# One row of a 128-row gather moved from GpSimd to SyncE, in a one-core GNN layer

## Chip, core and metric

The kernel runs on one core of one Trainium2 chip. The metric is device time in microseconds (us), the median of several executions. The core has five engines that run their own instruction streams: TensorE (PE, with its weight loads shown as PEld), VectorE (DVE), ScalarE (ACT), GpSimd (POOL) and SyncE (SP). They wait for each other through semaphores. SP, ACT and POOL also start DMA transfers, which run on 16 DMA engines.

## What is computed

The layer has 100,000 nodes with 32 features (`x`) and 25,000 edges, each with a source node `src`, a target node `dst` (sorted), four numbers `edge_attr_4` and eight numbers `edge_attr_8`.

```python
h = jnp.maximum(_layernorm(x, axis=-1), 0.0)
# per edge: an MLP of edge_attr_8 gives four 8x8 weight blocks
e = jax.nn.silu(edge_radial @ W1 + b1); e = jax.nn.silu(e @ W2 + b2); tpw = e @ W3 + b3
# messages: products of h[src], edge_attr_4 and tpw, summed over 8
agg = jax.ops.segment_sum(messages, dst, num_segments=n_atoms) / np.sqrt(AVG_NEI)
# self part: h through Ws and Wv
x = x + (h_self + agg)
```

So there is a dense part over all nodes (norm, ReLU, a small matrix, add to `x`, store) and a sparse part over the edges: fetch `x[src]` for each edge, normalise it, build 32 numbers per edge, and add them to the rows `dst` of the output.

## The kernel before, in words

**Tiles of edges.** The edges are cut into 196 tiles, 128 edges on 128 partitions each; the last one has 40 (`T` = 195 whole tiles, `TAIL` = 40, L54 to L59). The fetched rows of `x` stand in SBUF in `xg`, 32 numbers per partition and tile.

**Node stage**, until about 158 us. SP loads chunks of 2,048 nodes (`load_x`, L219), PE, ACT and DVE work on them, ACT stores them. At the same time POOL gathers rows of `x` for the edges.

**Edge stage**, from then on. PE, ACT and DVE work in 49 batches of four tiles. A batch ends with DVE's `idx_i`, the row numbers (L973), and ACT's copy of the sums into one of four buffers `sums` (L464). POOL then scatters each of the batch's four tiles with an indirect DMA that adds into the output (`scatter`, L319 to L340).

**POOL's order** (L298 to L349) is written out by hand. It gathers tiles 0 to 156 one after the other (`GA` = 157, L316), waits for the dense stores, and then, for each batch q, gathers tile 157 + q while that is under `G1` and scatters batch q:

```python
for q in range(NQ):
    if GA + q < G1:
        gather(GA + q)
    scatter(q, q)
```

A batch's first scatter is tile 3 of it, then come tiles 2, 1 and 0. The first waits until tiles 3, 2 and 1 of the batch before have landed, the second until its tile 0 has. ACT may overwrite a `sums` buffer only when POOL has passed that second point of a batch (`landed`, L335).

**SP's rows.** The last eight tiles, 188 to 195 (`RT` = 8, `G1` = 188), are not gathered by POOL. SP fetches each of their rows, 936 in all, by a DMA of its own of 128 bytes (`gather_rows`, L275 to L287). It first loads the row numbers into `row_i`, one DMA per tile (L266 to L270), and reads 32 of them at a time into registers. During the node stage it fetches four rows after each chunk load from the 13th chunk on, 144 in all, and the other 792 behind the last load.

**Who waits for gathered rows.** The first 120 tiles (`GF` = 120) are used in groups of ten in the node stage. The later ones are used in groups of seven, `late_tiles(v)`: DVE waits for a group in `late_landed(v)` (L1020), just ahead of the sum over its rows (L840). For groups 0 to 9 that is in the third batch of pass v, batch 4v + 2; the last group, tiles 190 to 195, is waited for at batch 44.

Of the kernel before, what the change touches and what calls it, by code (L numbers as in the profile page):

```python
# [20 lines left out]
def gnn_layer(nc, x, src, dst, edge_sh, edge_radial, W1, b1, W2, b2, W3, b3, Ws, Wv, out):  # L21
    f32, bf16, i32 = mybir.dt.float32, mybir.dt.bfloat16, mybir.dt.int32
# [3 lines left out]
    ds = bass.ds  # L26

    P = 128
    N, D = x.shape
# [24 lines left out]
    T = E // P  # L54
    TAIL = E - T * P
# [8 lines left out]

    GT, GL, GA, RT = 10, 7, 157, 8
    G1 = T + 1 - RT
    EW = UT * NB
    GF = EARLY * GT  # L70
    LATE = NU // 2 - 1
    assert 0 <= GF + GL * LATE - (T + 1) <= 1
    DR = D + 1
# [6 lines left out]
    src_main = src[0:T * P].rearrange("(p t) -> p t", p=P)  # L80
# [3 lines left out]
    with ctx:  # L84
        def sb(name, shape, dt=f32):
            return ctx.enter_context(nc.sbuf_tensor(name, shape, dt))

        def sem(name):
            return ctx.enter_context(nc.semaphore(name))
# [33 lines left out]
        nstd = sb("nstd", [P, 2, R])  # L123
        nrstd = sb("nrstd", [P, 2, R])

        row_i = sb("row_i", [1, RT * P], i32)
        src_all = sb("src_all", [P, T + 1], i32)
        xg = sb("xg", [P, (T + 2) * D])
        gsum = sb("gsum", [P, GT])
# [68 lines left out]
        src_loaded, row_loaded = sem("src_loaded"), sem("row_loaded")  # L198
        gathered = [sem(f"gathered{i}") for i in range(EARLY)]
        gathered_late = [sem(f"gathered_late{i}") for i in range(LATE)]  # L200
        gathered_row = [sem(f"gathered_row{i}") for i in range(RT)]

        def rows(ap, c, base):

            _, p, r = CH[min(base, NCH - 1)]
            r0 = c * (P * R) if base < FULL else CH[base][0]
            return ap[ds(r0, p * r), :].rearrange("(p r) d -> p (r d)", p=p), p, r * D
# [3 lines left out]
        def late_tiles(j):  # L211
            return range(GF + j * GL, min(GF + (j + 1) * GL, T + 1))

# [3 lines left out]
        @block.sync  # L217
        def _(sp):
            def load_x(c, base):  # L219
                if base >= XS:  # L220

                    sp.wait_ge(s["o_done"], c - XS + 1)
                v, p, n = rows(x, c, base)
                sp.dma_start(xin[0:p, base % XS, 0:n], v).then_inc(x_loaded[base % XS], 16)

            sp.dma_start(src_all[:, 0:T], src_main).then_inc(src_loaded, 16)
            for c in range(2):
                load_x(c, c)
            sp.wait_ge(s["selfw_zero"], 1)
            sp.dma_start(wself32[0:MUL, 0:MUL], Ws).then_inc(s["selfw_loaded"], 16)  # L230
            for i in range(3):
                with nc.allow_non_contiguous_dma(reason="64 weights"):
                    sp.dma_start(wself32[MUL + i:D:3, MUL + i:D:3], Wv).then_inc(s["selfw_loaded"], 16)
            for c in range(2, 4):
                load_x(c, c)
            sp.wait_ge(s["selfw_scaled"], 1)
            for g in range(4):
                sp.dma_start(wself[g * D:(g + 1) * D, g * D:(g + 1) * D], wself32[:, :]).then_inc(s["selfw_placed"], 16)
            sp.wait_ge(s["zeroed"], 1)
            for k in range(4):  # L240

                sp.wait_ge(s["xT_ready"], k + 1)
                load_x(k + 4, k + 4)
                if k == 0:

                    for h in range(2):
                        sp.dma_start(b3f[:, h * NTP:(h + 1) * NTP], b3.rearrange("(a n) -> a n", a=1)).then_inc(s["w_loaded"], 16)
                        sp.dma_start(w3blk[h * HR:(h + 1) * HR, h * NTP:(h + 1) * NTP], W3).then_inc(s["w_loaded"], 16)
                if k == 1:
                    for h in range(2):  # L250
                        sp.dma_start(w2blk[h * HR:(h + 1) * HR, h * HR:(h + 1) * HR], W2).then_inc(s["w_loaded"], 16)
                        sp.dma_start(b1col[h * HR:(h + 1) * HR, :], b1.rearrange("(n a) -> n a", a=1)).then_inc(s["w_loaded"], 16)
                        sp.dma_start(b2col[h * HR:(h + 1) * HR, :], b2.rearrange("(n a) -> n a", a=1)).then_inc(s["w_loaded"], 16)
                if k == 2:
                    sp.dma_start(dst_i[:, 0:T], dst_main).then_inc(s["dst_loaded"], 16)
                    sp.dma_start(sh_all[:, 0:T * 4], sh_main).then_inc(s["sh_loaded"], 16)
                for t in (2 * k, 2 * k + 1):
                    sp.dma_start(w1big[t * NB:(t + 1) * NB, t // 2, (t % 2) * HR:(t % 2 + 1) * HR], W1)\
                      .then_inc(s["w_loaded"], 16)
            sp.dma_start(er_all[:, 0:T * NB], er_main).then_inc(s["er_loaded"], 16)  # L260
            sp.dma_start(er_all[0:TAIL, T * NB:(T + 1) * NB], edge_radial[T * P:E, :]).then_inc(s["er_loaded"], 16)
            sp.dma_start(sh_all[0:TAIL, T * 4:T * 4 + 4], edge_sh[T * P:E, :]).then_inc(s["sh_loaded"], 16)
            sp.wait_ge(s["dst_pad"], 1)
            sp.dma_start(dst_i[0:TAIL, T:T + 1], dst[T * P:E].rearrange("(n a) -> n a", a=1)).then_inc(s["dst_loaded"], 16)

            for t in range(G1, T + 1):  # L266
                n = P if t < T else TAIL
                rows_of = src_main[:, t:t + 1].rearrange("p a -> a p") if t < T else src_tail.rearrange("n a -> a n")
                with nc.allow_non_contiguous_dma(reason="128 row numbers"):
                    sp.dma_start(row_i[:, (t - G1) * P:(t - G1) * P + n], rows_of).then_inc(row_loaded, 16)  # L270
            sp.dma_start(out[N:N + BT * P, :].rearrange("(p r) d -> p (r d)", p=P), spare0[:, :]).then_inc(s["spare_stored"], 16)

            late_rows = iter([(t, p) for t in range(G1, T + 1) for p in range(P if t < T else TAIL)])
            nodes = []

            def gather_rows(count):

                for t, p in itertools.islice(late_rows, count):
                    if p % 32 == 0:
                        o = (t - G1) * P + p  # L280
                        w = min(32, (P if t < T else TAIL) - p)
                        _, numbers = nc.values_load_multi_w_load_instructions(
                            row_i[0:1, o:o + w], engines=[mybir.EngineType.SP], min_val=0, max_val=N - 1,
                            skip_runtime_bounds_check_because="src holds rows of x")
                        nodes[:] = numbers
                    sp.dma_start(xg[p:p + 1, t * D:(t + 1) * D], x[ds(nodes[p % 32], 1), :])\
                      .then_inc(gathered_row[t - G1], 16)  # L287

            for c in range(XS, NCH):
                load_x(c, c)  # L290
                if c == 12:
                    sp.wait_ge(row_loaded, 16 * RT)
                if 12 <= c < FULL:
                    gather_rows(4)
            gather_rows(P * RT)


        @block.gpsimd  # L298
        def _(pool):
# [10 lines left out]

            def gather(t):
                signal = gathered[t // GT] if t < GF else gathered_late[(t - GF) // GL]
                pool.indirect_dma_start(xg[:, t * D:(t + 1) * D], None, x,  # L313
                                        bass.IndirectOffsetOnAxis(ap=src_all[:, t:t + 1], axis=0)).then_inc(signal, 16)

            pool.wait_ge(src_loaded, 16)  # L316
            for t in range(GA):
                gather(t)
# [33 lines left out]
        def _(act):  # L352
# [192 lines left out]
            edge_pass(0, True, False, True)  # L545
            with act.Fori(1, LATE - 1) as v:
                edge_pass(v, False, False, True)
            edge_pass(LATE - 1, False, False, False)
            edge_pass(LATE, False, True, False)
            copy_sums(NQ - 2, NQ - 2)  # L550
# [188 lines left out]
        def _(dve):  # L739
# [280 lines left out]
            def late_landed(v):  # L1020
                tiles = late_tiles(v)
                dve.wait_ge(gathered_late[v], 16 * len([t for t in tiles if t < G1]))
                for t in tiles:
                    if t >= G1:
                        dve.wait_ge(gathered_row[t - G1], 16 * (P if t < T else TAIL))

            def edge_pass(v, first, last):
                n = EARLY + v
                t0 = GF + v * GL
                was, ww = ((EARLY - 1) * GT, GT) if first else (t0 - GL, GL)  # L1030
                for h in range(2):
# [8 lines left out]
                    for r in range(2):  # L1040
# [3 lines left out]
                        products(q, k, u)  # L1044
                        if h == 1 and r == 0 and v < LATE - 1:
                            late_landed(v)
# [74 lines left out]
```

## Time and profile before

| what | value |
|---|---|
| median of 3 runs | 618.04 us (617.47 to 618.76) |
| the profiled execution | 617.0 us |
| its span, first to last instruction | 615.0 us |
| busy: PE / DVE / ACT / POOL | 529.1 / 463.4 / 389.3 / 488.3 us |
| POOL's 196 scatters, 188 gathers | 305.7 us, 181.6 us busy |
| mean granted TensorE clock | 0.824 of full speed |

The span leaves out 2.0 us of the profiled execution's own time. A busy engine is not always the one that sets the end; the chain of waits tells which one does. DMA packets are counted per queue: q0 is the one that POOL's indirect DMAs use, q1 that of SP.

### The profile page before, as it was taken

The numbers are of one execution on the slowest core, as the hardware profiler recorded it, in microseconds if no ns is written. First come the engines' busy times: TensorE is split into PE (matmuls) and PEld (weight loads), VectorE is DVE, ScalarE is ACT, GpSimd is POOL, SyncE is SP. The second block draws the span as 40 slices with busy tenths as digits, with TensorE's granted clock in tenths as the row PEclk, the third lists the DMA queues.
The fourth block names the chain that finished last, engine by engine and source line by source line (L and its number), as shares of the span: only waits on it lengthen the run. The fifth ranks groups of instructions, "written<-read, shape, count | busy, mean of one in ns | idle before, by whom it ended". The sixth has DMA issues, their size and how long they took to land.

```text
span 615.0 us, 12788 instructions
## 1 busy us (share of the span) xinstructions
PE 529.1 (86%) x2843; PEld 394.7 (64%) x2867; DVE 463.4 (75%) x1125; ACT 389.3 (63%) x1103; POOL 488.3 (79%) x393
## 2 busy tenths in 40 slices
PE   6979999999799999888897998889899999987700
PEld 4768888888556666656664766566565666654600
DVE  4678889898489997777787777768877788857700
ACT  3426565656477977767596757757785778776400
POOL 6777777777777888888888888888888787888787
PEclk9959999999697887777888777778877778787755
DMA  4756667664200122222222222222222222222222
GB/s 129 193 184 185 203 195 203 207 204 141 82 14 15 12 11 12 11 10 10 12 11 11 11 10 13 9 11 10 12 10 11 11 8 10 10 10 9 10 9 9
DMA packets 53524, 34.36 MB, mean 56 GB/s; under 512 B 37062, under 2 KB 40920, under 8 KB 53464
## 3 DMA queue, kind: packets, MB, share of 16 engines
q0 software_dynamic: 34240, 6.32, 18.0%
q1 hardware_dynamic: 12054, 14.60, 8.2%
q10 hardware_dynamic: 7170, 12.81, 5.7%
q8 instruction: 18, 0.29, 0.2%
q14 instruction: 42, 0.34, 0.2%
HBM read 17.59 MB, written 16.08 MB: 55 GB/s over the span
## 4 chain that ended last, share of the span: by engine, by line
POOL 64%; issue 21%; DMA 14%; POOLq 0%
POOL out_dram L325 38%; POOL xg L313 25%; DMA out_dram<-sums,idx_i 14%; DMA src_all<-in_src_dram 0%; POOLq L335 0%; POOLq L341 0%; POOLq L342 0%; POOLq L331 0%
## 5 line engine op out<-in xcount | busy, mean ns | idle before, releaser
L325 POOL DMA_INDIRECT out_dram<-sums,idx_i x196 | 305.7, 1560 | 65.6 <-issue 54.4
L313 POOL DMA_INDIRECT xg<-in_x_dram,src_all x188 | 181.6, 966 | 58.4 <-issue 57.0
L645 PE MATMUL ps<-w3blk,x 128*128 128x512 f32 x196 | 142.5, 819 | 1.6 <-issue 0.4
L692 PE MATMUL ps<-msg,eq 128*128 128x32 f32 (+1 forms) x980 | 124.7, 287 | 1.8 <-DVE msg L1014 1.8
L692 PEld LDWEIGHTS ps<-msg,eq 128*128 128x128 f32 x980 | 124.4, 207 | 2.1 <-DVE msg L1014 2.0
L994 DVE TENSOR_REDUCE red<-prod 128x128 f32<-128x1024 f32 x49 | 97.8, 1996 | 0.1
L476 ACT ACTIVATE dsq<-ps,dcol 128x512 f32<-128x512 f32 x196 | 87.1, 537 | 0.2 <-PE ps L657 0.2
L464 ACT ACTIVATE sums<-ps 128x132 f32<-128x132 f32 x49 | 13.7, 279 | 111.6 <-POOLq L335 87.7
L645 PEld LDWEIGHTS ps<-w3blk,x 128*128 128x128 f32 x196 | 46.9, 253 | 44.4 <-issue 40.8
L498 ACT ACTIVATE eq<-dsq,onecol 128x384 f32<-128x384 f32 x147 | 73.4, 519 | 0.0
L657 PEld LDWEIGHTS ps<-ident,dcol 128*128 128x128 f32 x196 | 25.4, 151 | 59.1 <-issue 57.0
L596 PEld LDWEIGHTS ps<-ones_g,sqT 128*128 128x128 f32 x392 | 52.5, 202 | 12.8 <-issue 11.7
L602 PE MATMUL ps<-wself,rT 128*128 128x128 f32 x392 | 58.7, 295 | 0.0
L949 DVE SCALAR_TENSOR_TENSOR first<-sums,rank_max,dmt_all 128x4 f32<-128x4 f32 x49 | 10.8, 221 | 62.4 <-ACT sums L464 62.3
L376 ACT ACTIVATE sqT<-ps 128x512 f32<-128x512 f32 (+2 forms) x50 | 29.3, 585 | 44.4 <-PE ps L587 44.1
L981 DVE TENSOR_TENSOR prod<-ps,coef 128x768 f32<-128x768 f32 x49 | 46.8, 954 | 11.7 <-PE ps L646 9.3
L657 PE MATMUL ps<-ident,dcol 128*128 128x128 f32 x196 | 32.4, 292 | 26.1 <-ACT dsq L476 26.1
L985 DVE TENSOR_TENSOR prod<-ps,coef 128x256 f32<-128x256 f32 x147 | 52.8, 415 | 0.0
L1001 DVE TENSOR_REDUCE msg<-prod 128x32 f32<-128x512 f32 x49 | 52.5, 1072 | 0.0
L602 PEld LDWEIGHTS ps<-wself,rT 128*128 128x128 f32 x392 | 50.2, 200 | 0.1
L596 PE MATMUL ps<-ones_g,sqT 128*128 128x4 f32 x392 | 49.5, 249 | 0.4 <-DMA wself<-wself 0.4
L626 PE MATMUL ps<-erT,w1big 64*128 64x128 f32 x196 | 43.8, 389 | 3.7 <-ACT erT L404 3.1
(106 smaller groups left out, 803.9 us busy)
## 6 DMA issues: line engine op xcount, KB each, us to landing
xg<-in_x_dram SPq DMA_DIRECT2D x936, 0.1 KB
xin<-in_x_dram SPq DMA_DIRECT2D x48, 256.0 KB, 3.0
out_dram<-oc ACTq DMA_DIRECT2D x48, 256.0 KB, 2.3
out_dram<-sums,idx_i POOLq DMA_INDIRECT x196, 3.0
xg<-in_x_dram,src_all POOLq DMA_INDIRECT x188, 2.4
er_all<-in_edge_attr_dram SPq DMA_DIRECT2D x1, 780.0 KB
sh_all<-in_edge_attr_dram SPq DMA_DIRECT2D x1, 390.0 KB
xin<-in_x_dram SPq DMA_DIRECT2D x1, 192.0 KB, 3.1
```

What stands on the lines that cost most here:

```text
L313: pool.indirect_dma_start(xg[:, t * D:(t + 1) * D], None, x, bass.IndirectOffsetOnAxis(ap=src_all[:, t:t + 1], axis=0)).then_inc(signal, 16)
L325: pool.indirect_dma_start(out, bass.IndirectOffsetOnAxis(ap=idx_i[:, k % NS, a:a + 1], axis=0), sums[:, k % NS, a * DR:a * DR + D], None, ...
L476: m = act.activation(dsq[:, b * BW:b * BW + (BT - b) * P], psDT[:, b * P:BW], ACT.Square, bias=dcol[:, k % NS, b:b + 1], scale=-1.0)
L498: m = act.activation(e[:, o], dsq[:, o], ACT.Relu, bias=onecol[:, :], scale=-4.0, accum_out=lcnt[:, k % NS, b:b + 1])
L596: m = pe.matmul(psV[base % 2][0:p, 4 * g:4 * g + 4], sqT[:, base % 2, g * P:g * P + p], ones_g[:, :], start=True, stop=True)
L602: m = pe.matmul(psY[base % 2][0:p, g * P:(g + 1) * P], rT[:, base % 2, g * P:g * P + p], wself[:, :], start=True, stop=True)
L645: pe.matmul(o, x2[:, k // 2 % 2, j * P:(j + 1) * P], w3blk[:, :], start=True, stop=False)
L657: m = pe.transpose(psDT[:, b * P:(b + 1) * P], dcol[:, k % NS, b:b + 1].to_broadcast([P, P]), ident[:, :])
L692: m = pe.matmul(psSUM[:, a * DR:a * DR + n], eq[:, k % 2, o:o + P], msg[:, k % 2, b, 0:n], start=(b == a), stop=(b == a - 1 and (a < BT - ...
L985: m = dve.tensor_tensor(prod[:, :, 192 + 64 * i:256 + 64 * i].rearrange("p t (g w) -> p t g w", w=MUL), w[:, :, 192:256].rearrange("p t (g ...
L994: dve.tensor_reduce(red[:, :, :, :], prod[:, :, 128:384].rearrange("p t (g u w) -> p t g w u", u=MUL, w=MUL), X, ALU.add).then_inc(s["red_ ...
L1001: dve.tensor_reduce(msg[:, k % 2, :, 0:MUL], prod[:, :, 0:128].rearrange("p t (u w) -> p t w u", w=MUL), X, ALU.add)
```

## The change

Tiles 0 to 119 are gathered as before. From tile 120 on (the 121st), POOL's gather covers 127 partitions instead of 128. The 128th row of each of these tiles is fetched by SP, as a single-row DMA. SP's share of whole tiles shrinks from eight to seven (tiles 189 to 195), so POOL gathers tile 188 too: 189 gathers instead of 188, of which 69 have 127 rows. The 69 row numbers come with one more load into `row_i`; one load of 128 row numbers falls away. SP fetches the 69 single rows ahead of its whole tiles. SP has 877 rows in all. DVE has one more wait in `late_landed`.

```diff
-    GT, GL, GA, RT = 10, 7, 157, 8
+    GT, GL, GA, RT = 10, 7, 157, 7
     G1 = T + 1 - RT
     EW = UT * NB
     GF = EARLY * GT
+    ONES = G1 - GF
...
-        row_i = sb("row_i", [1, RT * P], i32)
+        row_i = sb("row_i", [1, RT * P + ONES], i32)
...
+        gathered_one = [sem(f"gathered_one{i}") for i in range(LATE)]
...
+            sp.dma_start(row_i[:, RT * P:RT * P + ONES], src_main[P - 1:P, GF:G1]).then_inc(row_loaded, 16)
+
+            ones = [(t, P - 1, RT * P, t - GF, ONES) for t in range(GF, G1)]
+            rows_of_tiles = [(t, p, (t - G1) * P, p, P if t < T else TAIL)
+                             for t in range(G1, T + 1) for p in range(P if t < T else TAIL)]
+            late_rows = iter(ones + rows_of_tiles)
...
-                for t, p in itertools.islice(late_rows, count):
-                    if p % 32 == 0:
+                for t, p, o, i, n in itertools.islice(late_rows, count):
+                    if i % 32 == 0:
...
-                    sp.dma_start(xg[p:p + 1, t * D:(t + 1) * D], x[ds(nodes[p % 32], 1), :])\
-                      .then_inc(gathered_row[t - G1], 16)
+                    sp.dma_start(xg[p:p + 1, t * D:(t + 1) * D], x[ds(nodes[i % 32], 1), :])\
+                      .then_inc(gathered_row[t - G1] if t >= G1 else gathered_one[(t - GF) // GL], 16)
...
-                    sp.wait_ge(row_loaded, 16 * RT)
+                    sp.wait_ge(row_loaded, 16 * (RT + 1))
...
-            gather_rows(P * RT)
+            gather_rows(ONES + P * RT)
...
-                pool.indirect_dma_start(xg[:, t * D:(t + 1) * D], None, x,
-                                        bass.IndirectOffsetOnAxis(ap=src_all[:, t:t + 1], axis=0)).then_inc(signal, 16)
+                n = P if t < GF else P - 1
+                pool.indirect_dma_start(xg[0:n, t * D:(t + 1) * D], None, x,
+                                        bass.IndirectOffsetOnAxis(ap=src_all[0:n, t:t + 1], axis=0)).then_inc(signal, 16)
...
                 dve.wait_ge(gathered_late[v], 16 * len([t for t in tiles if t < G1]))
+                dve.wait_ge(gathered_one[v], 16 * len([t for t in tiles if t < G1]))
```

## Rows read from the trace of the kernel before

**Rows 1.** The page: the span's chain that ended last, shares by engine.

```profile
POOL 64%; issue 21%; DMA 14%; POOLq 0%
```

**Rows 2.** Timeline of POOL: start us, length us, what [idle before <-releaser]. Early gathers.

```profile
194.71 0.95 POOL L313 DMA_INDIRECT xg<-in_x_dram,src_all  x1 [0.30 <-issue]
195.97 0.95 POOL L313 DMA_INDIRECT xg<-in_x_dram,src_all  x1 [0.30 <-issue]
...
202.28 1.63 POOL L325 DMA_INDIRECT out_dram<-sums,idx_i  x1 [0.30 <-issue]
```

**Rows 3.** Timeline of POOL: one batch, from its gather to the next scatter.

```profile
218.59 1.02 POOL L313 DMA_INDIRECT xg<-in_x_dram,src_all  x1 [0.30 <-issue]
219.91 1.57 POOL L325 DMA_INDIRECT out_dram<-sums,idx_i  x1 [0.30 <-DMA out_dram<-sums,idx_i]
221.79 1.56 POOL L325 DMA_INDIRECT out_dram<-sums,idx_i  x1 [0.30 <-issue]
223.66 1.56 POOL L325 DMA_INDIRECT out_dram<-sums,idx_i  x1 [0.30 <-issue]
...
227.37 1.02 POOL L313 DMA_INDIRECT xg<-in_x_dram,src_all  x1 [0.30 <-issue]
```

**Rows 4.** Timeline of POOL: the first batch without a gather, and the last scatter.

```profile
471.45 1.55 POOL L325 DMA_INDIRECT out_dram<-sums,idx_i  x1 [0.30 <-issue]
473.31 1.55 POOL L325 DMA_INDIRECT out_dram<-sums,idx_i  x1 [0.30 <-issue]
475.70 1.55 POOL L325 DMA_INDIRECT out_dram<-sums,idx_i  x1 [0.84 <-issue]
...
611.52 1.55 POOL L325 DMA_INDIRECT out_dram<-sums,idx_i  x1 [0.30 <-issue]
```

**Rows 5.** Waits between 210 and 470 us: who for whom, total us, times, longest.

```profile
ACT sums L464 <- POOLq L335: 70.9, 29, 3.6
```

**Rows 6.** The page: DMA queue of POOL's indirect DMAs: packets, MB, share of 16 engines.

```profile
q0 software_dynamic: 34240, 6.32, 18.0%
```

**Rows 7.** Timeline of POOL: its smallest instruction, a fill of one column.

```profile
0.26 0.10 POOL L1109 MEMSET const-float32-0.0<- 128x1 f32 x1 [0.26 <-issue]
```

**Rows 8.** Timeline of DVE: the row numbers of batches 0, 1 and 2.

```profile
185.83 0.16 DVE L973 TENSOR_TENSOR idx_i<-idx_f,trash 128x4 int32<-128x4 f32 x1
...
197.20 0.15 DVE L973 TENSOR_TENSOR idx_i<-idx_f,trash 128x4 int32<-128x4 f32 x1
...
204.64 0.16 DVE L973 TENSOR_TENSOR idx_i<-idx_f,trash 128x4 int32<-128x4 f32 x1
```

**Rows 9.** Stretches: window, us, busy PE, PEld, DVE, ACT, POOL, granted clock, DMA share, GB/s.

```profile
175.00:180.00 5.00, 4.64 (x23) 2.62 (x21) 4.93 (x8) 3.72 (x9) 3.78 (x5) 1.00 0.08 13
...
210.00:470.00 260.00, 238.39 (x1120) 167.03 (x1133) 205.62 (x508) 188.69 (x560) 214.86 (x149) 0.80 0.23 11
```

**Rows 10.** Gathers and their readers: what touches xg (duration min/median/max ns, first and last start), and landing.

```profile
L313 POOL DMA_INDIRECT xg<-in_x_dram,src_all x188: 947/952/1189, 3.1 to 464.5; - x188
L840 DVE TENSOR_REDUCE gsum<-xg x12: 374/377/428, 157.2 to 537.9; 128x7 f32<-128x224 f32 x11, 128x10 f32<-128x320 f32 x1
...
DMA to landing us min/median/max: 2.2/2.4/3.3
```

**Rows 11.** Timeline of DVE: row sums of group 0 and of group 9.

```profile
187.78 0.37 DVE L840 TENSOR_REDUCE gsum<-xg 128x7 f32<-128x224 f32 x1
...
490.49 0.38 DVE L840 TENSOR_REDUCE gsum<-xg 128x7 f32<-128x224 f32 x1
```

**Rows 12.** Timeline of SP's queue: number loads, the 18th four rows, the last 792.

```profile
23.16 6.31 SPq L270 DMA_DIRECT2D row_i<-in_src_dram  x8
...
88.85 1.46 SPq L286 DMA_DIRECT2D xg<-in_x_dram  x4
...
141.92 382.85 SPq L286 DMA_DIRECT2D xg<-in_x_dram  x792
```

More of the change, by code:

```diff
@@ L271, in _ @@
             sp.dma_start(out[N:N + BT * P, :].rearrange("(p r) d -> p (r d)", p=P), spare0[:, :]).then_inc(s["spare_stored"], 16)
-            late_rows = iter([(t, p) for t in range(G1, T + 1) for p in range(P if t < T else TAIL)])
+            sp.dma_start(row_i[:, RT * P:RT * P + ONES], src_main[P - 1:P, GF:G1]).then_inc(row_loaded, 16)
[3 more added lines that the diff above has]
+            late_rows = iter(ones + rows_of_tiles)
             nodes = []
             def gather_rows(count):
-                for t, p in itertools.islice(late_rows, count):
-                    if p % 32 == 0:
-                        o = (t - G1) * P + p
-                        w = min(32, (P if t < T else TAIL) - p)
+                for t, p, o, i, n in itertools.islice(late_rows, count):
+                    if i % 32 == 0:
+                        w = min(32, n - i)
                         _, numbers = nc.values_load_multi_w_load_instructions(
-                            row_i[0:1, o:o + w], engines=[mybir.EngineType.SP], min_val=0, max_val=N - 1,
+                            row_i[0:1, o + i:o + i + w], engines=[mybir.EngineType.SP], min_val=0, max_val=N - 1,
                             skip_runtime_bounds_check_because="src holds rows of x")
                         nodes[:] = numbers
-                    sp.dma_start(xg[p:p + 1, t * D:(t + 1) * D], x[ds(nodes[p % 32], 1), :])\
-                      .then_inc(gathered_row[t - G1], 16)
+                    sp.dma_start(xg[p:p + 1, t * D:(t + 1) * D], x[ds(nodes[i % 32], 1), :])\
+                      .then_inc(gathered_row[t - G1] if t >= G1 else gathered_one[(t - GF) // GL], 16)
             for c in range(XS, NCH):
```

## The prediction

> **What bounds the kernel now.** I read the chain of waits first. It runs through POOL nearly from end to end: 64% are POOL's own instructions and 21% the gaps between them, and the DMA part of 14% is the landing of scatters, which mostly runs beside POOL's next instructions [rows 1]. PE is busier in sum (529.1 us against 488.3), but sums don't tell which engine ends last, so I looked at POOL's timeline. In the first 200 us it is one gather after the other, 0.95 us each and 0.30 us to the next, so one gather every 1.26 us [rows 2]. Then a batch is one gather and four scatters, 1.32 us and 4 x 1.87 us, together 8.78 us from gather to gather, again with no more than the 0.30 us between instructions [rows 3]. There are 31 such batches, then 18 without a gather, until the last scatter starts at 611.52 [rows 4]. The other engines run ahead and are held back by POOL: between 210 and 470 us ACT waits 29 times, 70.9 us in all, until POOL frees a buffer [rows 5], some 2.4 us a batch. So a microsecond taken from POOL's sequence should be a microsecond of the kernel, as long as that reserve lasts, and one added costs one.
>
> **The change, part by part.**
>
> *The tile that POOL takes over (188).* It is gathered ahead of batch 31. At today's price that is 1.32 us [rows 3]. Batch 31 now idles 0.84 us ahead of its second scatter, 0.54 us more than the usual 0.30 [rows 4]: it waits for the scatter started at 471.45 to land. A gather in between covers that. Net +0.8 us.
>
> *The 69 gathers of 127 rows.* They are tiles 120 to 188: 37 in the early sequence and 32 ahead of batches 0 to 31. No row shows a gather of 127 rows. If the price goes by rows, each saves 1/128 of 0.95 us, 0.007 us, 0.5 us in all. What may change more is how the transfer is split. The queue has 34,240 packets [rows 6]; 188 gathers of 32 packets and 196 scatters of 144 make exactly that number. So I read a gather as 16 packets with 8 rows each and 16 small ones that signal the end, one of each per DMA engine, and a scatter as 128 row packets and 16 signals. 128 rows divide into 16 equal shares; 127 is a prime, so a program that wants equal shares must put all rows on one DMA engine. POOL would then prepare one list, not sixteen.
>
> Bounds for a gather: it can't cost less than POOL's smallest instruction, 0.10 us [rows 7], a saving of 0.85 us; above, I take the scatter, 1.56 us for the same 128 rows handled as separate packets [rows 3], 0.61 us more than a gather. Between these ends I choose an estimate. The scatter's 0.61 us over 128 rows is 4.8 ns per row for handling a row on its own. If the basic work on a row is about as much, 128 rows take 0.61 us of the gather; 0.10 us is the floor of any instruction; 0.24 us of the 0.95 are left for setting up 16 lists, 15 ns each. One list instead of 16 then saves 15/16 of 0.24 us, and with the row about **0.23 us a gather**. 69 x 0.23 = 15.9 us.
>
> The trace's packet count can't tell what 127 rows do. [...]
>
> *Landing of a gather on one DMA engine.* Between 175 and 180 us only gathers and single rows move: a DMA share of 0.08 of 16 engines, 6.4 engine-us for four gathers, at most 1.6 each [rows 9]. All on one engine, that adds 1.6 us to a landing of 2.4 [rows 10]. Group 9, the one with the tightest distance, is summed by DVE at 490.5 us [rows 11], and its last POOL gather would start at 473 us at today's pace: nobody waits. If instead the rows went as single packets like the scatter's: 0.23 x 16 x 260 us over 29.6 batches is 32 engine-us a batch [rows 9], some 8 for each scatter of 144 packets, 0.056 us a packet, so 7.1 us on one engine. A scatter behind it on that engine would land late. The scatter that must have landed by the next batch's first one starts 5.1 us after the gather, the next batch's first scatter 10.1 us after it; the rows would be through by some 8 us. Cost nothing; if a row took over 0.07 us, POOL would wait.
>
> *SP.* One number load more and one less, 0.79 us each [rows 12], in a stretch where SP waits for DVE anyway. 69 rows come first and fit in the 144 that SP fetches during the node stage (the 18 groups of four that they take are through at 90.3 us [rows 12]); their first reader, the sum of group 0, runs at 187.8 us [rows 11]. In all SP has 877 rows, not 936. 733 are left at 141.9 us, at 382.85/792 = 0.483 us each: SP ends at 496 us, not 525 [rows 12]. The last group is summed at 537.9 us [rows 10], some 15 us earlier after the change: 27 us of reserve, against 13 us before. Cost nothing.
>
> *DVE's added wait.* Eleven waits on semaphores that were raised long before; what stands behind them on DVE is a row sum of 0.38 us [rows 10]. Under 0.1 us each, and DVE is not the bound.
>
> *Does POOL find its work?* The early savings bring it to its first scatter 38 x 0.23 = 8.7 us earlier, 193.5 instead of 202.28 [rows 2]; the row numbers of batch 0 are there at 186.0 [rows 8]. Batch 1's scatters then begin at 202.1 (numbers at 197.4), batch 2's at 210.6 (204.8). Batches of 8.55 us leave ACT 2.2 us of its 2.4 us wait. Up to 0.3 us a gather nothing is lost here. At 0.5 us POOL would reach its first scatter at 183.3 and wait 2.7 us for batch 0 and 3.2 us for batch 1.
>
> *Sum:* +0.8 - 15.9 = -15.1 us. 617.0 - 15.1 = 601.9 us for the profiled execution; the median stands 1.0 us above that one, so **603 us**.
>
> **Rivals.**
>
> (a) *The price goes by rows.* For it: nothing in the trace shows a set-up per DMA engine. Then the added tile and 69 x 0.007 us nearly cancel: +0.3 us, 618.3. Chance 0.15.
>
> (b) *127 rows take a slower path on POOL, and the kernel is slower.* 128 rows over 16 engines may be the case for which POOL's program works on 16 lists at once; 127 rows on one list, or in unequal shares, would be handled row by row. For it: the scatter, which costs 0.61 us more for the same rows, so a slower path exists. Against: what is slow there may be the adding. Place: each of the 69 gathers, 37 of them before the first scatter. Price up to 69 x 0.61 = 42 us: 617.0 + 0.8 + 42.1 = 659.9, with the 1.0 us **661 us**. It decides from 0.03 us a gather on, where 69 x 0.03 and the 0.8 make 2.9 us. Chance 0.25, with anything between 620 and 661 us or beyond.
>
> (c) *The gathers get much cheaper and the gain stops at the other engines.* With 0.5 us a gather: +0.8 - 34.5 + 5.9 = -27.8 us, 590 us, the rest lost in the two waits for row numbers. Against more: PE is busy 92% of the 260 us at a clock of 0.80 [rows 9]. Chance 0.1.
>
> **How the numbers follow.** The forecast has 0.5, rival (c) 0.1, (a) 0.15 and (b) 0.25. A change under 0.2%, 1.2 us, can't be told from none here. Of (a) some lands on either side: faster 0.60, same 0.13, slower 0.27. The range must leave out no more than 0.2: it takes in (c) at 590 with a little below, 587, the forecast and (a), and the beginning of (b), up to 0.1 us a gather dearer, 618 + 0.8 + 6.9 = 626. What is left out is most of (b).
>
> **What would show it.** In the profile after: POOL's 69 gathers of tiles 120 on at about 0.72 us early and 0.79 later, the 120 others at 0.95. Queue q0 with fewer packets for them. Batch to batch 8.55 us, first scatter near 193.5 us, SP's last row near 496 us, no wait of DVE ahead of the sums of `xg`. If those gathers show 0.95 us, (a) holds; over that, (b); if POOL idles ahead of batches 0 and 1 for `idx_i`, (c). The forecast is wrong in another way if the gathers are cheaper and the batches still take 8.8 us, with POOL waiting for landings.

## The result and the profile after

The kernel became slower, by 127.8 us: a median of 745.7 us (744.65 to 746.25, 4 runs) against 617.94 us. The ratio is 1.2058, with a 95% interval from 1.2039 to 1.2078. The forecast was 603 us, the range ended at 626 us, and the rival on the slow side was priced at up to 661 us.

The page of the kernel after: its span, the chain's shares, then POOL's two groups of instructions (busy us, mean ns, idle ahead of them). Lines of this kernel are shifted: the scatter is L333, the gather L321, and L343 is where POOL signals that a buffer is free.

```profile
span 743.5 us, 12621 instructions
POOL 68%; issue 27%; DMA 4%; POOLq 0%
L333 POOL DMA_INDIRECT out_dram<-sums,idx_i x196 | 306.6, 1564 | 66.4 <-issue 61.7
L321 POOL DMA_INDIRECT xg<-in_x_dram,src_all x189 | 291.9, 1545 | 74.9 <-issue 73.0
```

The chain still runs through POOL, as it did before [rows 1]. The scatters cost nearly what they did (305.7 us before), but the gathers went from 181.6 to 291.9 us busy. POOL's timeline shows where. First the last 128-row gather and the first two with 127 rows (tiles 120 and 121), then the seventh of these and the eighth (tiles 126 and 127), then the first scatter:

```profile
153.08 0.95 POOL L321 DMA_INDIRECT xg<-in_x_dram,src_all  x1 [0.30 <-issue]
154.34 2.56 POOL L321 DMA_INDIRECT xg<-in_x_dram,src_all  x1 [0.30 <-issue]
157.20 2.55 POOL L321 DMA_INDIRECT xg<-in_x_dram,src_all  x1 [0.30 <-issue]
...
171.68 2.54 POOL L321 DMA_INDIRECT xg<-in_x_dram,src_all  x1 [0.31 <-issue]
177.84 2.55 POOL L321 DMA_INDIRECT xg<-in_x_dram,src_all  x1 [3.62 <-issue]
...
279.01 1.65 POOL L333 DMA_INDIRECT out_dram<-sums,idx_i  x1 [0.30 <-issue]
```

A gather of 127 rows takes 2.54 us, one of 128 rows 0.95 us. In the batches they take 2.59 and 1.02 us. Besides, POOL stands still for 3.6 us instead of 0.30 ahead of tile 127, and again ahead of 134, 141, 148 and 155. The first scatter starts at 279.01 us, not 202.28 [rows 2]. One batch, in the rows that answer to [rows 3]:

```profile
286.56 2.59 POOL L321 DMA_INDIRECT xg<-in_x_dram,src_all  x1 [0.30 <-issue]
289.47 1.59 POOL L333 DMA_INDIRECT out_dram<-sums,idx_i  x1 [0.32 <-issue]
...
296.96 2.59 POOL L321 DMA_INDIRECT xg<-in_x_dram,src_all  x1 [0.30 <-issue]
```

10.4 us from gather to gather instead of 8.78, and no stalls here.

So the 128.5 us by which the span grew are these. The 38 slow gathers ahead of the first scatter: 38 x 1.59 = 60.4. The 31 behind it: 31 x (2.59 - 1.02) = 48.7. Five stalls, 16.3 us together. Tile 188 at its old price, 1.3 us by a run below. That makes 126.7; 1.8 us are left over, about half of it in scatters that are a little longer (306.6 us in all, not 305.7) and the rest in small gaps.

What the other engines did meanwhile: the longest waits (who for whom, total us, times, longest), and the stretch from 210 to 260 us (busy us of PE, PEld, DVE, ACT, POOL, then clock, DMA share, GB/s).

```profile
ACT sums L472 <- POOLq L343: 219.4, 39, 67.9
DVE first L957 <- ACT sums L472: 188.4, 42, 66.1
```

```profile
210.00:260.00 50.00, 0.10 (x1) 0.00 (x0) 0.00 (x0) 0.00 (x0) 39.06 (x16) 0.53 0.38 8
```

ACT's wait for POOL in [rows 5] was 70.9 us; here ACT once waits 67.9 us in one piece. The three compute engines filled the four buffers and then did next to nothing for these 50 us, with POOL alone at work.

The queue q0, and SP's last fetches (start, length, count):

```profile
q0 software_dynamic: 37584, 6.85, 25.7%
```

```profile
141.34 379.54 SPq L293 DMA_DIRECT2D xg<-in_x_dram  x733
```

The packets tell how a gather is made. In the trace of the kernel before, q0's packets have three sizes: 3,008 of 1,024 bytes, which is 16 for each of 188 gathers, with 8 rows of 128 bytes in each; 25,088 of 128 bytes, 128 for each of 196 scatters; and 6,144 of 4 bytes, 16 for each of the 384 transfers. In 35 of the 37 gathers of tiles 120 to 156 a 4-byte one is the last packet ahead of the next gather, and the last of the 16 steps of the gather's semaphore stands 0.28 to 0.64 us behind the last 4-byte one (30 gathers, those with all 16 steps in the trace), so the 4-byte ones are read as signals.

In the kernel after, 120 gathers of 32 packets and 196 scatters of 144 leave 5,520 packets for the 69 gathers of 127 rows, 80 each. By their sizes these 80 are (bytes; the second column is how they are read):

```
3 x 4096, 1 x 3968   : 127 rows of 128 bytes, in packets of 32, 32, 32 and 31
45 x 128, 15 x 124   : 15 times 127 pieces of 4 bytes, in packets of 32, 32, 32 and 31
16 x 4               : the 16 signals
```

A sixteenth of the packets that are not signals, four of 64 here, is called a list, and a row or a 4-byte piece in it an entry. One list holds all rows: its four packets come one behind the other, and in none of the 69 gathers do two of them overlap by more than 7 ns, while of the 124-byte packets up to 15 are under way at once. The trace does not name the DMA engine of a packet, so the prediction's "one of each per DMA engine" and its one engine for 127 rows are shown only as far as these times go. The sizes of the others read as 15 lists filled up to the same length of 127 with pieces of 4 bytes. The profile shows packets and not the pieces in them, so the 4 bytes are inferred from the sizes. The bytes agree: q0 moved 0.53 MB more than in [rows 6], 7.7 KB for each of 69 gathers, and 15 x 127 x 4 bytes are 7.6 KB. Where a 128-row gather has 8 entries in each of 16 lists (1,024 bytes each), this one has, by this reading, 127 in each of 16.

### The profile page after: what moved, and what is told of

Read it like the earlier page. It is cut to its first block, busy times and chain, and to the rows that moved or that the text cites. A ratio compares the mean times of both kernels' runs of the same rounds, so it can differ in the third digit from the quotient of the medians.

```text
span 743.5 us, 12621 instructions
## 1 busy us (share of the span) xinstructions
PE 567.2 (76%) x2843; PEld 425.7 (57%) x2867; DVE 464.1 (62%) x1125; ACT 389.2 (52%) x1103; POOL 599.5 (81%) x394
## 4 chain that ended last, share of the span: by engine, by line
POOL 68%; issue 27%; DMA 4%; POOLq 0%
POOL out_dram L333 35%; POOL xg L321 33%; DMA out_dram<-sums,idx_i 4%; DMA src_all<-in_src_dram 0%; POOLq L343 0%; POOLq L349 0%; POOLq L339 0%; POOLq L350 0%
## 5 line engine op out<-in xcount | busy, mean ns | idle before, releaser
L333 POOL DMA_INDIRECT out_dram<-sums,idx_i x196 | 306.6, 1564 | 66.4 <-issue 61.7
L321 POOL DMA_INDIRECT xg<-in_x_dram,src_all x189 | 291.9, 1545 | 74.9 <-issue 73.0
L653 PE MATMUL ps<-w3blk,x 128*128 128x512 f32 x196 | 146.9, 842 | 2.1 <-issue 1.1
L700 PEld LDWEIGHTS ps<-msg,eq 128*128 128x128 f32 x980 | 145.6, 237 | 2.1 <-DVE msg L1022 1.8
L700 PE MATMUL ps<-msg,eq 128*128 128x32 f32 (+1 forms) x980 | 145.3, 312 | 1.6 <-DVE msg L1022 1.1
L665 PE MATMUL ps<-ident,dcol 128*128 128x128 f32 x196 | 35.2, 310 | 119.3 <-ACT dsq L484 119.3
L653 PEld LDWEIGHTS ps<-w3blk,x 128*128 128x128 f32 x196 | 48.9, 264 | 47.7 <-issue 44.1
L634 PE MATMUL ps<-erT,w1big 64*128 64x128 f32 x196 | 46.9, 411 | 3.4 <-ACT erT L412 3.1
```

The source lines that it names most:

```text
L321: pool.indirect_dma_start(xg[0:n, t * D:(t + 1) * D], None, x, bass.IndirectOffsetOnAxis(ap=src_all[0:n, t:t + 1], axis=0)).then_inc(signa ...
L333: pool.indirect_dma_start(out, bass.IndirectOffsetOnAxis(ap=idx_i[:, k % NS, a:a + 1], axis=0), sums[:, k % NS, a * DR:a * DR + D], None, ...
L653: pe.matmul(o, x2[:, k // 2 % 2, j * P:(j + 1) * P], w3blk[:, :], start=True, stop=False)
L665: m = pe.transpose(psDT[:, b * P:(b + 1) * P], dcol[:, k % NS, b:b + 1].to_broadcast([P, P]), ident[:, :])
L700: m = pe.matmul(psSUM[:, a * DR:a * DR + n], eq[:, k % 2, o:o + P], msg[:, k % 2, b, 0:n], start=(b == a), stop=(b == a - 1 and (a < BT - ...
```

## The experiments

All of them start from the kernel before. Those with fewer rows per gather leave SP's part as it was before (eight whole tiles, no single rows). The rows left out stay at zero in `xg`, so their share of the edges is computed from zeros. For that DVE clears these tiles at the start, and POOL waits for it once, at the latest ahead of the first of them. The diffs leave these lines out, and so they do added semaphores and DVE's waits for them.

**rt7_only: only the eighth tile moved.** `RT = 7`, all gathers with 128 rows.

```diff
-    GT, GL, GA, RT = 10, 7, 157, 8
+    GT, GL, GA, RT = 10, 7, 157, 7
```

> The kernel before with SP's whole tiles cut from eight to seven and nothing else: POOL gathers 189 tiles, all with 128 rows. Both theories: the added gather costs 1.32 us less the 0.54 us of idle time ahead of batch 31's second scatter that it covers, so +0.8 us, 618.7 us against 617.9. If it costs over 3 us, a part of the 128 us of the change is not in the 127-row gathers.

Measured: 619.1 us against 617.8, ratio 1.0025 (1.0010 to 1.0039), 1.3 us more. POOL's timeline where the added gather stands:

```profile
473.65 1.02 POOL L313 DMA_INDIRECT xg<-in_x_dram,src_all  x1 [0.30 <-issue]
474.97 1.57 POOL L325 DMA_INDIRECT out_dram<-sums,idx_i  x1 [0.30 <-DMA out_dram<-sums,idx_i]
476.85 1.56 POOL L325 DMA_INDIRECT out_dram<-sums,idx_i  x1 [0.30 <-issue]
```

The gather costs 1.32 us with its gap, and the 0.84 us ahead of the second scatter is gone, as said. The interval of the ratio is 0.6 to 2.4 us and takes in the expected 0.8, so whether the 0.54 us of covered idle time were won can't be told. Moving the tile is about 1% of the loss.

**no_single_rows: 127 rows without SP's part.**

```diff
+                n = P if t < GF else P - 1
...
-                pool.indirect_dma_start(xg[:, t * D:(t + 1) * D], None, x,
-                                        bass.IndirectOffsetOnAxis(ap=src_all[:, t:t + 1], axis=0)).then_inc(signal, 16)
+                pool.indirect_dma_start(xg[0:n, t * D:(t + 1) * D], None, x,
+                                        bass.IndirectOffsetOnAxis(ap=src_all[0:n, t:t + 1], axis=0)).then_inc(signal, 16)
```

> The kernel before with POOL's 68 gathers from tile 120 on cut to 127 rows; SP fetches eight whole tiles as before and no single rows, so the last row of those tiles is left at zero. Theory A (the change's loss is all in POOL's preparation of 127-row gathers): 2.54 and 2.59 us a gather instead of 0.95 and 1.02, five stalls of 3.3 us among the first 37, one such gather fewer than in the change: 745.7 - 2.9 + 0.5 = 743 us, within 2 us. Theory B (SP's single-row DMAs or their landings take part in it): under 738 us.

Measured: 741.35 us (739.75 to 744.97), ratio 1.2017 (1.1985 to 1.2050). The loss is there without a single-row DMA. This run has one slow gather fewer than the change, 2.9 us. Of the 4.35 us between the two medians some 1.5 us are then left for SP's 69 rows and all else, and runs that spread from 739.75 to 744.97 us don't tell that from nothing.

**row_counts: ten sizes in one trace.**

```diff
+    COUNTS = 4 * [112] + 4 * [120] + 4 * [126] + 4 * [125] + 4 * [124] + 4 * [96] + 4 * [64] + 3 * [127] + 3 * [122] + 3 * [32]
...
+                n = COUNTS[(t - GF) % len(COUNTS)] if t >= GF else P
```

> One trace with many sizes: from tile 120 on POOL gathers, in turn, 4 tiles each of 112, 120, 126, 125, 124, 96 and 64 rows, then 3 each of 127, 122 and 32; the rows above are left at zero. Theory A (the rows go in k equal lists, k the largest number up to 16 that divides them, and POOL pays 13.4 ns per entry of the longest list, from 2.54 - 0.95 us over 127 - 8 entries): 112 rows 0.94 us, 120 (15 lists of 8) 0.95, 126 (14 of 9) 0.97, 125 (5 of 25) 1.18, 124 (4 of 31) 1.26, 96 0.93, 64 0.90, 127 2.54, 122 (2 of 61) 1.66, 32 0.87 us. Theory B (any number that 16 does not divide takes a path that handles each row by itself): 120, 122, 124, 125, 126 and 127 all between 2.4 and 2.6 us, the others near 0.95. Stalls of 3.3 us: by A none, since the lists stay short.

POOL's timeline, one row for each size: 112, 120, 126, 125, 124, 96, 64, 127, 122 and 32 rows in this order.

```profile
156.66 0.92 POOL L317 DMA_INDIRECT xg<-in_x_dram,src_all  x1 [0.30 <-issue]
...
160.79 0.97 POOL L317 DMA_INDIRECT xg<-in_x_dram,src_all  x1 [0.30 <-issue]
...
165.90 0.99 POOL L317 DMA_INDIRECT xg<-in_x_dram,src_all  x1 [0.30 <-issue]
...
169.75 1.18 POOL L317 DMA_INDIRECT xg<-in_x_dram,src_all  x1 [0.30 <-issue]
...
177.30 1.27 POOL L317 DMA_INDIRECT xg<-in_x_dram,src_all  x1 [0.30 <-issue]
...
182.24 0.91 POOL L317 DMA_INDIRECT xg<-in_x_dram,src_all  x1 [0.30 <-issue]
...
189.55 0.91 POOL L317 DMA_INDIRECT xg<-in_x_dram,src_all  x1 [0.30 <-issue]
191.97 2.55 POOL L317 DMA_INDIRECT xg<-in_x_dram,src_all  x1 [0.30 <-issue]
...
200.52 1.66 POOL L317 DMA_INDIRECT xg<-in_x_dram,src_all  x1 [0.30 <-issue]
...
206.41 0.87 POOL L317 DMA_INDIRECT xg<-in_x_dram,src_all  x1 [0.30 <-issue]
```

The whole kernel took 632.5 us, measured once. Theory A gave 0.94, 0.95, 0.97, 1.18, 1.26, 0.93, 0.90, 2.54, 1.66 and 0.87 us. All ten rows shown are within 0.02 us; 128 and 127 rows had gone into the law, the other sizes had not. Of the 27 other gathers of these sizes ahead of the batches two stand out, at 1.36 us (120 rows) and 1.48 us (124 rows), and in the batches a gather costs some 0.05 us more, as it does at 128 rows. Theory B, a slow path for every number that 16 does not divide, needed 2.4 us or more at 120 and 126 rows, where 0.97 and 0.99 us were measured, and fell. The packet sizes in this trace agree with the number of lists. A list is one packet, at 122 rows two (packets x bytes for one gather, without the signals):

```
rows  with rows                 filler
128   16 x 1024 (8 rows)
120   15 x 1024 (8 rows)         1 x 32
126   14 x 1152 (9 rows)         2 x 36
125    5 x 3200 (25 rows)       11 x 100
124    4 x 3968 (31 rows)       12 x 124
122    2 x 4096, 2 x 3712 (61)  14 x 128, 14 x 116
```

A list of filler has in each case 4 bytes for every row in a list of rows. Gathers of 112, 96, 64 and 32 rows have 16 packets of 896, 768, 512 and 256 bytes. Of the packets with rows at most 5 were under way at once at 125 rows, 4 at 124 and 2 at 122.

**rows_122: a second price on the same line, in the whole kernel.** The edit of no_single_rows with `n = 122` from tile 120 on.

> POOL gathers 122 rows from tile 120 on (two lists of 61), the rows above left at zero, eight whole tiles on SP. If POOL pays per entry of the longest list, each of the 68 gathers costs 1.66 us, 0.71 us more than at 128 rows: 48 us, 617.8 + 48 = 666 us without stalls. If seven 127-row gathers stall because 7 x 128 entries fill something, gathers of 62 entries stall after each 14th, ahead of tiles 134 and 148, some 6 us: 672 us. If the stalls come with the change of the semaphore once gathers are slow: ahead of 127, 134, 141, 148 and 155, some 16 us: 682 us.

Measured: 666.9 us against 617.4, ratio 1.0802 (1.0767 to 1.0837): 49.5 us more, where 68 x 0.71 = 48 us were expected, and no stall where the other two readings put one. The 15th of these gathers, tile 134:

```profile
181.93 1.66 POOL L316 DMA_INDIRECT xg<-in_x_dram,src_all  x1 [0.30 <-issue]
```

122 rows cost 50 us and 127 rows cost 124. So the number of rows has little to do with it; the length of the lists has: 1.66 us a gather with 61 entries, 2.54 with 127.

**The stalls.** They are 16 us of the loss. The profile names nothing that releases POOL there (its word is `issue`). Five runs, all with 127 rows, changed where the slow gathers begin, or which semaphore they signal.

*start_at_123*: `n = P if t < GF + 3 else P - 1`.

> 127 rows only from tile 123 on, the last row of those tiles left at zero, eight whole tiles on SP. It tells apart what the stalls of 3.3 us after each seventh gather hang on. Theory A (the room of the descriptor lists: seven gathers fill it): the first stall stands ahead of tile 130, then 137, 144, 151. Theory B (the change of the semaphore, which comes with each group of seven tiles): ahead of tiles 127, 134, 141, 148, 155. Gathers 120 to 122 at 0.95 us. Time by A about 743 - 3 x 1.6 - one stall of 3.3 = 735 us.

Measured once: 733.5 us. No stall ahead of tile 127 and none ahead of 130; the first stands ahead of 134, behind eleven slow gathers, then every seven:

```profile
186.49 2.54 POOL L316 DMA_INDIRECT xg<-in_x_dram,src_all  x1 [0.31 <-issue]
193.18 2.54 POOL L316 DMA_INDIRECT xg<-in_x_dram,src_all  x1 [4.15 <-issue]
```

Neither theory was right as put.

*two_semaphores*: 127 rows from tile 120 on; the first three gathers of a group signal one semaphore, the other four another.

```diff
-                signal = gathered[t // GT] if t < GF else gathered_late[(t - GF) // GL]
+                signal = gathered[t // GT] if t < GF else (gathered_late if (t - GF) % GL < 3 else gathered_tail)[(t - GF) // GL]
```

> 127 rows from tile 120 on, last row left at zero, eight whole tiles on SP, and in each group of seven the first three gathers signal one semaphore and the other four another. If a change of the semaphore makes POOL stall: stalls ahead of tiles 123, 127, 130, 134 and so on, some ten of 3.3 us, 741 + 17 = 758 us. If it is a matter of how much has been put into the lists: stalls ahead of 127, 134, 141, 148, 155 as before, 741 us.

Measured once: 727.4 us, no stall at all, though the same entries went into the same lists. More changes of the semaphore made fewer stalls. Both expectations missed again. POOL's gathers of tiles 126 and 127:

```profile
175.05 2.55 POOL L317 DMA_INDIRECT xg<-in_x_dram,src_all  x1 [0.30 <-issue]
177.91 2.54 POOL L317 DMA_INDIRECT xg<-in_x_dram,src_all  x1 [0.30 <-issue]
```

*start_at_116*: `n = P if t < GF - 4 else P - 1`.

> 127 rows from tile 116 on, last row left at zero, eight whole tiles on SP, semaphores as they were (groups of ten below tile 120, of seven above). If the stalls count what has been put into the lists, the pattern of seven moves: with 11 gathers between tile 123 and the stall ahead of tile 134 in the run that started there, and 7 in the ones that started at 120, what counts is a running total over all gathers, and the stalls need not stand ahead of 127, 134, 141. If they hang on the groups: ahead of 120 or 127, then 134, 141, 148, 155. Four more slow gathers, 4 x 1.6 us: 741 + 6 = 747 us, one stall more or less 3.3 us.

Measured once: 747.1 us, as expected by the count of gathers. No stall ahead of 120, and none ahead of 123, the eighth slow gather; the first one stands ahead of 127, behind eleven slow gathers, then every seven:

```profile
183.91 2.55 POOL L316 DMA_INDIRECT xg<-in_x_dram,src_all  x1 [3.51 <-issue]
```

*cut_groups*: the groups are cut at 6, 5, 7, 6, 5.

> 127 rows from tile 120 on as in the run with two semaphores, but the groups of seven are cut at other places: 6 + 1, 5 + 2, 7 (uncut), 6 + 1, 5 + 2, later ones 4 + 3. So far a stall of 3.3 us stood behind each run of seven slow gathers on one semaphore (change, tiles 120 on) and behind none of 3 + 4. If it takes seven in a row on one semaphore: one stall only, behind the uncut group, ahead of tile 141, 727.4 + 3.3 = 731 us. If six are enough: also ahead of 126 and 147, 737 us; if five: four or five stalls, 741 us or more. If none stands anywhere, the link to the semaphores is wrong.

Measured once: 728.2 us. POOL's rows ahead of tile 127 (6 + 1), tile 141 (the uncut group) and tile 148 (6 + 1):

```profile
175.02 2.55 POOL L318 DMA_INDIRECT xg<-in_x_dram,src_all  x1 [0.95 <-issue]
...
218.04 2.54 POOL L318 DMA_INDIRECT xg<-in_x_dram,src_all  x1 [3.47 <-issue]
...
238.32 2.54 POOL L318 DMA_INDIRECT xg<-in_x_dram,src_all  x1 [0.66 <-issue]
```

The full stall, 3.47 us, stands behind the uncut group alone. Behind 6 + 1 there is a rest of it, 0.95 and 0.66 us, and behind 5 + 2 nothing, 0.30 us. The rest ends 6.34 us after the sixth gather started (168.68), which is about what the full stalls have after their seventh (171.68 to 177.84 is 6.16).

Landings show what ends these waits. In the kernel after, tile 126's gather started at 171.68 us and had landed 5.4 us later, at 177.10, and POOL went on at 177.84; behind its other four stalls POOL went on 0.60 us after the seventh gather's landing. In cut_groups it went on 0.71 us after the landing of the sixth gather (174.31) and not of the seventh (176.94, after POOL had gone on), which signals another semaphore. In all 22 waits of the kernel after, no_single_rows, start_at_123, start_at_116 and cut_groups, POOL went on 0.58 to 0.74 us after the last gather of the seven, or of the six, that signal one semaphore had landed. Where the run is shorter, it has landed before POOL gets there: in two_semaphores the third gather, tile 122, had landed at 166.29 us, and tile 127 started at 175.05 with the usual 0.30 us ahead of it.

A count fits all these places: seven gathers of 127 rows may stand in it and not eight; ahead of the eighth, the oldest run of gathers that signal one semaphore must have landed, and then leaves the count as a whole. That the count is one of room in the lists is the author's guess; no run shows it. In the batches, where no stall stands, scatters with other semaphores stand between the gathers, 10.4 us from one to the next. One run was made to test the count ahead of the fact.

*start_at_110*: `n = P if t < GF - 10 else P - 1`.

> 127 rows from tile 110 on, last row left at zero, eight whole tiles on SP; tiles 110 to 119 are one group of ten on one semaphore, then groups of seven. Two readings of the stalls. Room: the lists hold seven gathers of 127 rows (7 x 128 entries) and not eight, and POOL gets room back for whole runs of gathers that signal one semaphore, as far as they have landed; this fits all runs so far. Then seven gathers fill the lists in the middle of the group of ten: a stall ahead of tile 117, none ahead of 120 or 124, then ahead of 127, 134, 141, 148, 155; six stalls, and ten more slow gathers than from 120 on: 741.4 + 16 + 3 = 760 us. Bound: the stall belongs to the change of the semaphore: ahead of 120 and not ahead of 117, the others the same.

Measured once: 760.1 us. The rows around tiles 116 and 117, in the middle of the group of ten, and around 126 and 127:

```profile
158.73 2.54 POOL L316 DMA_INDIRECT xg<-in_x_dram,src_all  x1 [0.31 <-issue]
165.18 2.54 POOL L316 DMA_INDIRECT xg<-in_x_dram,src_all  x1 [3.91 <-issue]
...
191.50 2.54 POOL L316 DMA_INDIRECT xg<-in_x_dram,src_all  x1 [0.30 <-issue]
197.56 2.54 POOL L316 DMA_INDIRECT xg<-in_x_dram,src_all  x1 [3.52 <-issue]
```

The stall is where the count reaches eight, ahead of 117, with no change of the semaphore there, and none stands ahead of 120 or 124. The forecast of place and time held, and the six waits again end 0.60 to 0.74 us after the landing of the last gather before them. What POOL counts inside is not shown; the count is inferred from these places.

## Why the prediction was wrong

**What bounds the kernel: right, as far as it was put to the test.** POOL set the end before and after, and each microsecond added to its sequence was one of the kernel: 109 us of slower gathers and 16 us of stalls are 125 of the 128 us. Whether a microsecond taken away would have come out in full, no run shows.

**The tile that POOL takes over: right in place and gap.** +0.8 us was put down, 1.3 measured, with 0.8 inside the interval.

**The price of a 127-row gather: wrong, and this is the step that failed.** The prediction took the 0.95 us apart into 128 rows at 4.8 ns and 16 lists at 15 ns, and let one list instead of 16 save 0.23 us: 0.72 us a gather, where 2.54 was measured. The shares, 4.8 ns for a row and 15 ns for a list, were the author's estimate, and no run shows them. The run row_counts shows how the price goes: 0.87 us with 2 entries in the longest list (32 rows), 0.91 with 4 (64 rows), 0.95 with 8 (128 rows), 1.18 with 25 (125 rows), 1.27 with 31 (124 rows), 1.66 with 61 (122 rows), 2.55 with 127 (127 rows). A line through 0.95 and 2.54 us has 0.84 us at no entry and 13.4 ns for each, and all ten rows shown of that run are within 0.02 us of it. The packet sizes give 16 lists for every size. Going from 128 to 64 rows saves 0.04 us, where 4.8 ns a row would have given 0.3. Going from rows in 16 lists to rows in 1 leaves 16 lists and makes them 16 times as long: 127 - 8 = 119 entries, 1.59 us more. Over the 69 gathers the term was put at -15.9 us and came to +109.

**The bound was wrong for the same reason.** The scatter, 1.56 us, was taken as the dearest way to handle 128 rows. But a scatter is made otherwise, of 128 packets of 128 bytes, and it adds; no run shows what of its price is due to which. No gather in the trace before had lists longer than 8 (16 packets of 1,024 bytes each), so no row there could bound a list of 127. Rival (b) had the right sign and place, with a chance of 0.25, and 0.61 us for a price of 1.59. Its words, "handled row by row", are near what was measured but not it: the price goes with the length of the lists, and 122 rows, which 16 does not divide either, cost less than half of the extra time (0.71 us a gather, not 1.59). Even with the right price it lacked the 16 us of stalls, which the prediction had no term for and the trace before no row.

**How 127 rows are split: right for the rows, wrong for the lists.** All rows in one list is what the packets show, four of them one behind the other, but POOL did not then "prepare one list, not sixteen": the other 15 are there with filler, 60 packets of 124 and 128 bytes. That rows go in equal shares was an assumption of the prediction, and the ten sizes agree with it: 120, 126, 125, 124, 122 and 127 rows went in 15, 14, 5, 4, 2 and 1 lists, and 112, 96, 64 and 32 rows, like 128, in 16. What all rows on one DMA engine would cost was weighed only for the landing. The cost was in POOL's own instruction, 2.54 us and not 0.95.

**Landing: right that nobody waits, off in size.** A 127-row gather lands some 5.5 us after its start instead of 2.4; 4.0 was put down, and the 1.59 us by which POOL's instruction grew was not in it. What touches `xg` between 158 and 200 us, where all gathers have 127 rows, against [rows 10]:

```profile
DMA to landing us min/median/max: 5.4/5.5/5.8
```

DVE has no wait ahead of its sums.

**SP: right that it hides, off in size.** It ends at 520.9 us, not 496: a row took 379.54/733 = 0.518 us instead of 0.483. That comes with POOL's 127-row gathers and not with the single rows: in no_single_rows SP's 792 last rows took 411.96 us, 0.520 each. With POOL so late nobody noticed. At this pace, and with the last group summed at about 523 us as forecast, SP's reserve would have been 2 us and not 27.

## What to carry to other kernels

Ask of an indirect DMA from POOL how its rows divide, not how many they are: in the gathers here, with eleven row counts from 32 to 128, the rows went in as many lists as the largest number up to 16 that divides the count, and the price went with the length of a list, 13.4 ns an entry. Of the sizes tried here, 128, 120 and 112 rows are as good as each other (0.95, 0.97 and 0.92 us), 127 costs 2.7 times as much (2.54 us), and a row fetched needlessly costs less than a count that divides badly: 128 rows are 1.59 us cheaper than 127. An estimate that takes a price apart into unseen shares needs a trial of a second size first; one trace with ten sizes, which leaves rows out of the result, would have answered this one.

## What was not expected of the hardware

- The lists that get no rows are filled up to the length of the one that does, by the packet sizes with 4-byte entries: 80 packets for a 127-row gather, and 7.6 KB of filler for 16.3 KB of rows.
- One entry more in each of the 16 lists costs 13.4 ns, the rest of a gather 0.84 us, by the line through 0.95 us (8 entries) and 2.54 us (127). So a 32-row gather (0.87 us) is hardly cheaper than one of 128 (0.95 us).
- Seven gathers with lists of 127 that signal one semaphore are followed by a wait of 3.2 to 3.9 us, and with another split of the semaphores the wait is 0.4 to 0.7 us or none. Two semaphores instead of one took 14 us off a kernel of 741 us (one run of 727.4), without touching anything else. The wait ends 0.58 to 0.74 us after the landing of the last gather on that semaphore. Why POOL waits for it, no run shows.
